# A transformer layer with routed experts on one core: GpSimd's sixteen slot scatters are issued in three parts between the quarters of a normalisation

## What is computed

```python
mod = (silu(c) @ wmod)                       # six vectors of 512 per batch row: sa, ca, ga, sb, cb, gb
h = layernorm(x) * (1 + ca) + sa
x = x + ga * attention(h)                    # 16 heads of 32, causal softmax, then out @ w_o.T + b_o
h = layernorm(x) * (1 + cb) + sb
x = x + gb * ffn(h)

def ffn(h):                                  # 32 experts, capacity 256, hidden 256; top 4 of the best 4 groups
    scores = sigmoid(h @ gate_w.T)
    topk_idx, topk_w = route_tokens(scores, bias_corr)
    pos = running count of earlier tokens on the same expert
    routed = sum over k of topk_w * expert[topk_idx](h)      # dropped where pos >= 256
    shared = relu2(h @ shared_up_w.T) @ shared_down_w.T      # hidden 1024
    return routed + shared
```

## Time and profile before

| | us |
|---|---|
| Median of three runs | 2968.14 |
| Lowest and highest run | 2962.25, 2969.26 |
| Span of the profiled execution | 3027.5 |
| TensorE busy in it | 2895.4 (96%) |
| VectorE busy | 2179.3 (72%) |
| GpSimd busy | 1833.5 (61%) |
| ScalarE busy | 1341.6 (44%) |

### The profile page before, as it was taken

One profiled execution on the slowest core, in us unless ns is written; L12 is line 12 of the kernel. 1 busy time (PEld: TensorE's weight loads), 2 busy tenths in 40 slices (PEclk: granted clock), 3 DMA queues, 4 the chain that ended last, 5 costly groups with the idle time before them and its releaser, 6 DMA issues.

```text
span 3027.5 us, 49806 instructions
## 1 busy us (share of the span) xinstructions
PE 2895.4 (96%) x16480; PEld 2168.3 (72%) x16480; DVE 2179.3 (72%) x5344; ACT 1341.6 (44%) x2436; POOL 1833.5 (61%) x1077
## 2 busy tenths in 40 slices
PE   8999999999999999999999989999999999989997
PEld 5788888766666666666666677777777787767775
DVE  6555555678787878787877687777777787756664
ACT  2222222156666666666666522233222333226664
POOL 1233222278888888888886256766565666655664
PEclk9999999999999999999999999999999999999998
DMA  7655555756655665566555333332322322238996
GB/s 240 211 187 201 187 180 180 233 114 136 137 124 115 138 138 121 115 139 140 119 117 160 107 97 93 94 112 74 103 79 93 102 85 81 73 107 222 239 245 118
DMA packets 281948, 420.53 MB, mean 139 GB/s; under 512 B 48463, under 2 KB 132687, under 8 KB 281742
## 3 DMA queue, kind: packets, MB, share of 16 engines
q1 hardware_dynamic: 259214, 384.22, 44.9%
q0 software_dynamic: 22528, 33.72, 5.8%
HBM read 263.38 MB, written 153.01 MB: 138 GB/s over the span
## 4 chain that ended last, share of the span: by engine, by line
PE 53%; DVE 14%; POOL 14%; issue 8%; ACT 4%; DMA 4%; another core or an unknown queue 2%; DVEq 1%; POOLq 0%; SPq 0%; ACTq 0%
PE qkv_ps_m L840 12%; PE ffn_ps_m L2191 11%; POOL att_gathered L1105 6%; PE qkv_ps_m L844 6%; POOL att_pt L1098 5%; PE att_ps_o L1330 5%; PE att_ps_p L1386 4%; PE att_ps_s L1304 4%; DMA out<-exp_y,exp_tok_add 2%; PE exp_ps_u L1607 2%; PE exp_ps_y L1623 1%; PE att_ps_s L1361 1%; DVE ffn_att L147 1%; DVE ffn_x L149 1%
## 5 line engine op out<-in xcount | busy, mean ns | idle before, releaser
L247 DVE CUSTOM_DVE_ANT_0 att_ps_s<-att_ps_s,att_causal 128x512 f32<-128x512 f32 (+1 forms) x992 | 469.3, 502 | 175.5 <-PE att_ps_s L1304 171.3
L1166 ACT ACTIVATE att_pt<-att_ps_p 128x512 f32<-128x512 f32 (+1 forms) x1024 | 524.5, 589 | 143.6 <-PE att_ps_p L1389 110.2
L1304 PE MATMUL att_ps_s<-att_ks,att_qs 96*128 96x512 f32 x1488 | 513.4, 373 | 2.2 <-DVE att_lower L253 0.6
L1386 PE MATMUL att_ps_p<-att_qs,att_ks 98*128 98x512 f32 (+3 forms) x1536 | 498.5, 364 | 9.3 <-ACT att_pt L1166 8.0
L1098 POOL TENSOR_TENSOR att_pt<-att_pt 128x1024 f32<-128x1024 f32 (+2 forms) x153 | 331.1, 2164 | 166.6 <-PE att_ps_o L1330 144.8
L1105 POOL TENSOR_TENSOR att_gathered<-att_gathered,att_pt 128x2048 f32<-128x2048 f32 (+1 forms) x92 | 388.1, 4218 | 7.2
L1912 POOL DMA_INDIRECT slot_info<-ffn_info,ffn_slot x256 | 275.9, 1078 | 119.3 <-issue 76.5
L253 DVE TENSOR_REDUCE att_lower<-att_ps_s 128x1 f32<-128x512 f32 x496 | 339.2, 684 | 7.4 <-PE att_ps_s L1304 7.4
L1386 PEld LDWEIGHTS att_ps_p<-att_qs,att_ks 98*128 98x128 f32 x1536 | 272.6, 191 | 82.1 <-issue 34.7
L1304 PEld LDWEIGHTS att_ps_s<-att_ks,att_qs 96*128 96x128 f32 x1488 | 275.7, 191 | 73.3 <-DVE att_rowmax L247 27.7
L577 POOL TENSOR_TENSOR qkv_x<-qkv_x,qkv_mod 128x512 f32<-128x512 f32 x60 | 83.4, 1391 | 371.5 <-DVE qkv_x L671 371.5
(11 more groups left out here) (311 smaller groups left out, 6718.8 us busy)
## 6 DMA issues: line engine op xcount, KB each, us to landing
att_qs<-qk_parts SPq DMA_DIRECT2D x96, 512.0 KB, 6.8
att_ks<-qk_parts SPq DMA_DIRECT2D x96, 512.0 KB, 12.7
qk_parts<-qkv_out_hi SPq DMA_DIRECT2D x128, 256.0 KB, 2.2
qk_parts<-qkv_out_lo SPq DMA_DIRECT2D x128, 256.0 KB, 2.4
qkv_x<-x SPq DMA_DIRECT2D x16, 1024.0 KB, 5.6
v_rows<-qkv_out_v SPq DMA_DIRECT2D x64, 256.0 KB, 2.3
att_vs<-v_rows SPq DMA_DIRECT2D x32, 512.0 KB, 16.1
o_parts<-att_o SPq DMA_DIRECT2D x64, 256.0 KB, 7.9
```

The source lines that it names most:

```text
L247: dve.tensor_tensor_reduce(part, part, self.causal[:, UNIT - (c1 - c0):UNIT], scale=1.0, scalar=MASKED, op0=ALU.add, op1=ALU.max, accum_ou ...
L1166: act.activation(tile(c)[:, h, col:UNIT], ps_p[(NPROB * prev.g + n) % NP][:, col:UNIT], ACT.Exp, scale=float(HD) ** -0.5).then_inc(exp_don ...
L1304: pe.matmul(bank("s", cur.g, i)[:, 0:c1 - c0], qs[cur.slot][0:STACK, h, t * P:(t + 1) * P], ks[cur.slot][0:STACK, h, c0:c1], start=True, s ...
L1386: last = pe.matmul(part[:, i * (UNIT - col):(i + 1) * (UNIT - col)], ks[prev.slot][:, h + i, kt * P:(kt + 1) * P], qs[prev.slot][:, h + i, ...
```

## The change

GpSimd's `normalise` gets a function that is called ahead of each quarter. In the bodies of units 0 to 13 it issues five scatters of unit u ahead of the third quarter of unit u + 2 (j = 0 to 4) and five ahead of the fourth (j = 5 to 9); the six that are left follow the fourth. The wait for `slot_done` inside `scatter` stands in front of each part. The bodies of the last two units and the first normalisation (of unit 1, ahead of all bodies) are as before.

```diff
         SCATTERED_AHEAD = TOPK
+        SCATTERED = ((0, 5), (5, 10))
...
-            def normalise(u):
+            def normalise(u, before_part=lambda g: None):
 
                 pool.wait_ge(o_in, CREDIT + 16 * (1 + GH) * (u + 1))
                 pool.sem_inc(mark, 1)
                 for g in range(NG):
+                    before_part(g)
                     full = o_full[g % 2]
...
-                if half == 0 and not (isinstance(b, int) and b == LAST) or half == 1 and more:
-                    normalise(u + 2)
-                scatter(u, half, SCATTERED_AHEAD if u == UNITS - 2 else 0, UT * TOPK)
+                if b < LAST:
+                    normalise(u + 2, lambda g: scatter(u, half, *SCATTERED[g - 2]) if g >= 2 else None)
+                    scatter(u, half, SCATTERED[1][1], UT * TOPK)
+                else:
+                    scatter(u, half, SCATTERED_AHEAD if u == UNITS - 2 else 0, UT * TOPK)
```

## The result

The changed kernel takes **3024.1 us** (median of four runs, 3021.3 to 3028.1) where the kernel before, run beside it, takes 2968.7 (2962.3 to 2974.2). The ratio is 1.0184, with a 95% interval of 1.0165 to 1.0203: 55 us slower, against 35 predicted, and inside the range.

The account below looks back on a forecast made before the run. TensorE, busy 96%, was taken as the bound, so GpSimd's order matters only where TensorE waits. 14 units times 2.5 us gave 35 us on 2968, with clock loss and absorption set against each other: 3003 us, range 2970 to 3030.

Parts of the forecast that it names:

- GpSimd stands still 5.1 us: GpSimd idles 5.1 us between second and third quarter, waiting for the slots that VectorE computes.
- Slot block 2.66: VectorE's slot block takes 2.66 us instead of 5.67, as GpSimd is waiting meanwhile.
- First five scatters 6.4, the second five 7.14: GpSimd's scatters ahead of the third quarter take 6.4 us, those ahead of the fourth 7.14.
- Quarters 3.9 each: GpSimd's third and fourth normalisation quarters, now among VectorE's routing instructions, take 3.9 us each.
- TensorE waits 2.5 us: At each projection TensorE waits 2.5 us for the fourth quarter, in 14 units: 35 us.
- The clock adds 9 us: Behind the new wait at the projection, matmuls sometimes run at the 1.2 GHz level: 9 us added.
- The timed runs lack the old transpose waits: Timed runs mostly have short units, without the profiled transpose waits that could hide the new wait: cost 35 us.
- absorbed: Timed runs do have the profile's transpose waits, which hide part of the new wait: 16 us cost, 2984, chance 20%.
- Transpose waits should shrink: TensorE's waits at the token transposes behind the projection, 18.2 us in the profile, should shrink.
- what the faster slot block gives … costed at nothing: The quicker slot block frees 3.0 us of VectorE, which then waits for ScalarE: counted as nothing.
- VectorE late: In VectorE's routing steps, moved quarters block up to 3.0 us, even without a wait at the projection: 3000 us, chance 10%.
- The last rival: VectorE's chain behind the projection starts only 1.5 us behind the last scatter's new end: 58 us, 3026, chance 12%.

Follow-up runs that it names:

- 6, 6, 4: The changed kernel with six scatters ahead of the third quarter, six ahead of the fourth and four behind: 3043.7 us, ratio 1.0263.
- second profile: The kernel before, unchanged, profiled once more: span 2964.1 us, against 3027.5 in its first profile.
- 4, 4, 8: The changed kernel with four scatters ahead of the third quarter, four ahead of the fourth and eight behind: 3031.5 us, ratio 1.0217.
- 5, 0, 11: The changed kernel with five scatters ahead of the third quarter, none ahead of the fourth and eleven behind: 3031.5 us, ratio 1.0211.
- kernel without reads: The changed kernel with third and fourth quarters replaced by GpSimd fills that write the same buffers and read nothing: 2981.0 us, ratio 1.0048.
- 0, 10, 6: The changed kernel with no scatters ahead of the third quarter, ten ahead of the fourth and six behind: 2991.5 us, ratio 1.0077.

## Why the prediction was right, and where it was not

It was right in sign and within its range, and its main chain of events came about. But the nearness of 35 to 55 is partly luck, of two errors against each other: of the 35 us for the wait at the projection 14 x 1.05 = 15 came, while what the waits at the transposes cost, 2.63 us in most units and so at least 12 x 2.63 = 32, stands at nothing in the sum.

- *GpSimd stands still 5.1 us*: 5.04. *Slot block 2.66*: 2.64. *First scatter 0.86 behind the slots*: 0.86 (1902.37 - 1901.51). Right.
- *First five scatters 6.4, the second five 7.14*: 6.13 (1902.37 to 1908.50) and 6.50 (1912.14 to 1918.64). Both near their quick ends.
- *Quarters 3.9 each*: 3.48 and 3.94. *Switches 0.1 to 0.16*: 0.15. Together the queue's terms came out quicker than taken.
- *TensorE waits 2.5 us*: 1.05 in most units. The mechanism was right and the size too large by a factor of more than two. This follows from a wait being the small difference of long sums: 0.9 us less in the scatters and 0.4 in one quarter are most of it.
- *The clock adds 9 us*: it did not. Matmuls 0.43 us apart were found in the changed kernel behind one projection only (2240, where TensorE waited 3.9 less 0.2 us, and the granted clock from 2240.80 to 2243.00 was 0.50, the 1.2 GHz level). In the 6, 6, 4 kernel, with 3.5 us of wait, such stretches, seven matmuls or more, came in 11 of 13 units. Behind the waits of 1.05 us the matmuls were at full spacing (granted clock 1.00 from 1859.80 to 1862.00).
- *The timed runs lack the old transpose waits*: shown by the second profile. Of the prediction's arguments this one did most: it alone separates 3003 from the *absorbed* rival's 2984. The unit of the earlier trace rows, taken as one without a transpose wait, had one of 0.76 us for VectorE's low part; the usual period is 59.23, not 60.2.
- *Transpose waits should shrink*: **wrong**. 25.2 us of them appeared. The step that failed is "*what the faster slot block gives … costed at nothing*": the same edit that frees 3.0 us of VectorE in the slot block takes 5.0 from it in routing. The first is worth nothing, as VectorE then waits 3.50 us for ScalarE; the second was in the text only as a rival at 10%, "*VectorE late*", up to 3.0 us. That rival took the loss to be no larger than the one in the slot block, and it assumed that it came in place of a wait at P. Both came together.

The rival's own threshold holds well when worked out again. From L145 to the modulated tokens the chain takes 23.40 - 6.43 = 17.0 us in the changed kernel, and TensorE asks for them at P + 22.25. So L145 may start at P + 5.3. In the second profile of before it is at 3.5, with 1.8 us to spare. At 6.4, as in the change, 1.1 is late: 0.8 to 1.2 was measured. At 8.4, as in 4, 4, 8, it is 3.1: 2.9 was measured.

The sum over a unit of the changed kernel closes. The projection starts 1.05 late; from there the first tile's transpose starts at P + 23.40 instead of 22.25, the third's at 31.18 instead of 28.59, the fourth's at 34.40 instead of 31.77. 1.05 + 2.63 = 3.68 us, and the periods differ by 3.68 (62.91 and 59.23).

The wait at the third tile's transpose follows from VectorE's order. It writes into the buffer that the first tile's transpose used, so it needs VectorE's low part of the first tile, and that stands behind the additions of two down tiles. The first row is of before (its P is 1914.28), the second of the changed kernel (P is 1922.64):

```profile
1941.81 0.68 DVE L1993 TENSOR_TENSOR ffn_hT_lo<-ffn_ps_t,ffn_hT_hi 128x512 fp32r<-128x512 f32 x1
1953.30 0.68 DVE L1997 TENSOR_TENSOR ffn_hT_lo<-ffn_ps_t,ffn_hT_hi 128x512 fp32r<-128x512 f32 x1
```

It starts at P + 27.5 in before, ahead of the third transpose, and at P + 30.7 in the changed kernel, where TensorE goes on 0.14 us behind its end.

In 4, 4, 8 and 5, 0, 11, with 2.9 us of wait at the first transpose, this third wait came in 5 and 4 of 13 units. In each of the other 8 and 9, and in none of these, the matmuls behind the first transpose ran 0.43 us apart for a while (granted clock 0.50 from 1887.00 to 1888.00 in 4, 4, 8, and 1.00 in a unit with the third wait, 2014.50 to 2017.50). So the slower clock takes the place of the third wait there.

One sum in the rivals is off: the low end of the *absorbed* one (a wait of 1.8) comes out at 8.9 us, not 8.

The last rival's number, 3026, was the nearest to the truth, and its mechanism is false: in both kernels L145 starts before the scatters end (P + 6.4 and P + 8.0 in the changed one). A number that agrees doesn't confirm the story behind it.

Still open are two things: why the first profiled execution of before was 63 us longer, with pauses of VectorE ahead of L145 "remote" in the earlier trace rows, which the second doesn't have; and, as said, 9 us of the kernel without reads.

No order of these instructions that was tried beats the kernel before. There is a plain reason: in its second profile TensorE has next to no waits in this stretch (2.9 us), so GpSimd's order has nothing to give there.

## What to carry to other kernels

A GpSimd tensor instruction has two costs, its place in its own queue and the VectorE instruction that it falls on. When such work is moved, lay its new place over VectorE's timeline and mark the instructions with two SBUF inputs and the small copies, casts and additions of a scalar; count each GpSimd instruction there as one that may hold VectorE for its own length, even where the VectorE instruction is 0.2 us long. Before a wait in the profile is taken as slack to be used, compare the profiled span with the timed runs, and take a second profile where they differ by more than their spread.

## What the runs showed of the hardware

VectorE's small instructions are the ones that lose most. A product of 128 x 32 elements took 1.86 us beside a quarter and 0.19 with scatters or fills in its place; a cast of 16 elements a partition took 1.49 instead of 0.17, a TENSOR_SCALAR of 4 elements 1.79 instead of 0.44. Six GpSimd instructions cost VectorE 5.0 us per unit. A VectorE instruction can be held though the records have it start up to 0.48 us ahead of the GpSimd instruction (1908.03 and 1908.51 in the changed kernel). Fills by GpSimd, which write SBUF and read nothing, took 6.4 us per unit and lengthened none of the steps with two SBUF inputs beside them. One step with a single input, the TENSOR_SCALAR at 1974.38, took 0.59 us beside the last fill and ended with it.

The Trainium skill, SBUF — State Buffer, "Who interferes with whom", has this for steps with two inputs: a VectorE instruction with two SBUF inputs contends with a GpSimd instruction that reads SBUF, "not with one that only writes it". This case agrees, by the low part that took 1.80 beside the quarter (L2151) and 0.69 beside the fills (L2161). For a VectorE instruction in a two-port mode the page makes no such exception, and the 0.59 of the TENSOR_SCALAR beside a fill would fit that; but the profile doesn't show in which mode it ran.

Scatters of 128 pairs take 0.97 us each and 0.30 between when undisturbed, and up to 1.49 in before and 1.55 in 0, 10, 6, beside VectorE's routing. The switch from a tensor instruction to a scatter costs 0.15.
